# First weights in row halves, PSUM banks permuted, decode steps and x casts shared out anew

## What is computed

```
attn = einsum('ds,td->st', w1, w2) * sparse_mask
x = layernorm(x + gelu(x @ attn + b2))                 # exact gelu
e = norm(x, axis=-1);  mask = e > 64
y = where(mask, x @ W8.T, x @ W4.T) + bias             # W4, W8: weights decoded from bit planes by a table
x = layernorm(x + y)
```

## Time and profile before

| | us |
|---|---|
| median of 3 runs | 336.0 (335.06 to 337.29) |
| the profiled execution's own time | 336.07 |
| its span, first to last instruction | 334.3 |
| PE busy in it | 301.7 (90%) |
| DVE busy | 194.5 (58%) |
| ACT busy | 185.5 (55%) |
| POOL busy | 104.3 (31%) |
| granted PE clock, mean | 0.956 of full |

### The profile page before, as it was taken

How to read it: one execution, slowest core, us unless ns; L and a number is a source line. 1 busy time by engine, 2 the same in 40 slices (tenths; PEclk the granted TensorE clock), 3 DMA queues, 4 the chain that set the end, 5 groups by cost and what they waited for, 6 DMA issues and landing times.

```text
span 334.3 us, 5046 instructions
## 1 busy us (share of the span) xinstructions
PE 301.7 (90%) x1907; PEld 263.6 (79%) x1907; DVE 194.5 (58%) x347; ACT 185.5 (55%) x246; POOL 104.3 (31%) x179
## 2 busy tenths in 40 slices
PE   5899478989996779999999999999999999999970
PEld 2788375656664579999999999999999878878870
DVE  0668857436879577889966766640315434534361
ACT  1656653447887967897857887942124545121210
POOL 3000000322323237779888630000013232322220
PEclk9899877999997959999999999999999999999996
DMA  7999616799987592000111111111905877444232
GB/s 246 371 384 361 225 60 220 223 228 296 218 139 128 80 158 56 32 33 31 38 43 33 38 45 35 60 47 36 304 10 190 259 267 237 176 147 159 94 125 73
DMA packets 27183, 49.35 MB, mean 148 GB/s; under 512 B 2320, under 2 KB 11792, under 8 KB 27152
## 3 DMA queue, kind: packets, MB, share of 16 engines
q1 hardware_dynamic: 22800, 40.56, 35.0%
q0 software_dynamic: 4352, 8.39, 14.7%
HBM read 36.36 MB, written 12.58 MB: 146 GB/s over the span
## 4 chain that ended last, share of the span: by engine, by line
PE 64%; issue 12%; SPq 6%; POOL 6%; DMA 4%; DVE 3%; ACT 2%; POOLq 0%; DVEq 0%
PE acc L536 18%; PE acc L538 18%; PE acc L537 18%; POOL z L1329 5%; PE acc L519 4%; DMA q_low<-in_qbits 4%; SPq L250 3%; PE acc L461 2%; PE acc L451 1%; PE acc L415 1%; ACT x_hi L666 1%; SPq L254 1%; PE acc L431 1%; PE acc L433 0%; PE acc L432 0%
## 5 line engine op out<-in xcount | busy, mean ns | idle before, releaser
L536 PE MATMUL acc<-lin,zz 128*128 128x256 f32 (+2 forms) x424 | 130.9, 309 | 0.3 <-POOL lin L1337 0.3
L538 PE MATMUL acc<-lin,zz 128*128 128x256 f32 (+2 forms) x424 | 130.3, 307 | 0.0
L537 PE MATMUL acc<-lin,zz 128*128 128x256 f32 (+2 forms) x424 | 130.1, 307 | 0.0
L536 PEld LDWEIGHTS acc<-lin,zz 128*128 128x128 f32 x424 | 80.7, 190 | 4.7 <-issue 0.6
L537 PEld LDWEIGHTS acc<-lin,zz 128*128 128x128 f32 x424 | 80.8, 191 | 4.0
L538 PEld LDWEIGHTS acc<-lin,zz 128*128 128x128 f32 x424 | 80.7, 190 | 4.1
L692 ACT ACTIVATE leaf<-planes,lut,flip 128x1024 f32<-128x1024 uint8 x56 | 67.6, 1234 | 0.0
L948 DVE COPY_PREDICATED leaf<-planes,leaf 128x1024 f32<-128x1024 uint8 x32 | 43.1, 1346 | 12.5 <-ACT leaf L692 12.0
L1329 POOL DMA_DIRECT2D z<-in_xr x16 | 19.7, 1257 | 97.3 <-ACT z L674 97.3
L785 ACT ACTIVATE junk<-rows,cols 128x1024 bf16<-128x1024 f32 x15 | 17.2, 1149 | 41.3 <-POOL cols L1303 41.3
L415 PE MATMUL acc<-w,w 128*128 128x272 f32 (+1 forms) x128 | 31.5, 412 | 4.1 <-DMA w<-in_w1b 4.1
(11 more groups left out here) (105 smaller groups left out, 429.8 us busy)
## 6 DMA issues: line engine op xcount, KB each, us to landing
z<-in_xt SPq DMA_DIRECT2D x16, 512.0 KB, 8.8
z<-in_xr POOLq DMA_DIRECT2D x16, 512.0 KB, 6.9
out_rows<-rows SPq DMA_DIRECT2D x15, 512.0 KB, 2.9
w<-in_w2b SPq DMA_DIRECT2D x4, 1024.0 KB, 9.9
w<-in_w1b SPq DMA_DIRECT2D x8, 512.0 KB, 9.4
out_rows<-parts SPq DMA_DIRECT2D x32, 128.0 KB, 1.8
rows<-out_rows SPq DMA_DIRECT2D x16, 256.0 KB, 2.8
off_band<-in_mask_rest SPq DMA_DIRECT2D x8, 448.0 KB, 4.2
```

Source lines behind the costliest of these rows:

```text
L536: nc.tensor.matmul(bank, hi, w_hi, start=k == 0, stop=False)
L537: nc.tensor.matmul(bank, hi, w_lo, start=False, stop=False)
L538: last = nc.tensor.matmul(bank, lo, w_hi, start=False, stop=k == KB - 1)
```

## The change

**Loads (SP).** The first w2 part and w1 block 0 are each loaded in two halves by rows of the reduction (d 0 to 3, then 4 to 7), and strip 0 begins its first four products on the first halves. Between the halves stand the code bits of four blocks (256 KB, before: two blocks, 128 KB), the tables and b2. The first band half moves behind w1 block 1. The x pairs and the group-0 edge rows change their order; the loads of group 1 no longer wait for the masks, and those of groups 2 and 3 wait for the last strip alone. For this the band, the excess operands and the warm-up tile move in SBUF, from the place of z to that of `lin`; so the writes into `lin` (ACT, DVE, POOL) now wait until the masks and `mix_e` are done.

**PSUM.** UNIT_BANKS is (4, 5, 6, 7, 0, 1, 2, 3), STRIP_BANKS (2, 3). Units 0 and 1 now have the Gram banks, units 4 to 7 the banks of the linear parts. `turn(1)` uses banks 6 and 7.

**PE's order.** The excess strip comes before strip 7. Group 0 of the mix has the same order as the others; only its units 4 and 5 wait for `lin_lo` of block 0. `turn(1)` stands behind the whole mix. Then come the squares of three tiles, not one, before the first part; the squares of tile j+1 still precede part j from j = 2 on.

**ACT and DVE.** x casts of pairs 0 and 2 of group 0 go to DVE too; parts of group 0's x work move in between strips 5, 6 and 7. In the mix, the casts and decode steps stand at fixed places behind certain gelus. Counts:

| decode steps | before | after |
|---|---|---|
| among the strips | 22 | 24 |
| in the mix | 12 | 9 |
| first pass over the tiles | 32 | 33 |
| second pass | 31 | 30 (the last of before does nothing) |
| z pairs split in the mix | 6 | 4 |

The core of the diff, the counts and banks first:

```diff
-    STATS_AHEAD = 1
+    STATS_AHEAD = 3
-    EARLY_STEPS = [5, 2, 2, 2, 2, 3, 3, 3]
-    UNIT_STEPS = [n % 2 for n in range(18)] + [1, 1, 1, 0, 0, 0]
-    FIRST_STEPS = [2] * TILES
+    EARLY_STEPS = [6, 3, 3, 3, 3, 3, 2, 1]
+    MIX_STEPS = [(2, 1), (2, 1), (1, 0), (2, 0)]
+    MIX_Z = {2: ((0, 0), (0, 1)), 3: ((0, 2), (0, 3))}
+    FIRST_Z = [((1, 0), (1, 1)), ((1, 2),), ((1, 3),)] + [((2 + n // PAIRS, n % PAIRS),) for n in range(2 * PAIRS)] + [()] * 5
+    FIRST_STEPS = [1] + [2] * 11 + [3, 2, 3, 2]
...
-    TURN_IN_FIRST = {4: 2, 9: 3, 15: 4}
+    TURN_IN_FIRST = {5: 2, 11: 3, 15: 4}
...
-        UNIT_BANKS, GRAM_BANKS, SUM_BANK = (0, 1, 2, 3, 4, 7, 5, 6), (4, 5), 7
-        STRIP_BANKS, EXCESS_BANK = (5, 6), 7
+        UNIT_BANKS, GRAM_BANKS, SUM_BANK = (4, 5, 6, 7, 0, 1, 2, 3), (4, 5), 7
+        STRIP_BANKS, EXCESS_BANK = (2, 3), 7
```

SP, at the start:

```diff
+            load_first(slice(0, KB // 2), w_first)
+            load_q(0, slice(0, HALF_BLOCKS))
+            sp.dma_start(lut[:, :, :], lut4).then_inc(tables_loaded, 16)
+            sp.dma_start(b2[:, :], b2c).then_inc(tables_loaded, 16)
+            load_first(slice(KB // 2, KB), w_loaded[0])
+            load_w2(1)
+            load_w1(1)
+            load_band(0)
+            load_w1(2)
```

PE:

```diff
             for b in range(KB):
                 strip(b)
                 if b == TURN_AFTER_STRIP:
-                    turn_early(0)
-            excess_strip()
...
+                    pe.wait_ge(consts_made, 4)
+                    turn(0)
+                    excess_strip()
...
+            pe.wait_ge(gelu_done, KB * (GROUPS - 1) + 4)
+            turn(1)
```

ACT, in the mix:

```diff
+            for g in range(GROUPS):
+                gelu(g, 0)
+                done = decode_steps(MIX_STEPS[g][0], done)
+                if g + 1 < GROUPS:
+                    make_xe_hi(g + 1)
+                gelu(g, 1)
+                if g + 1 < GROUPS:
+                    make_x_hi(g + 1, 1)
+                gelu(g, 2)
+                gelu(g, 3)
+                for pair in MIX_Z.get(g, ()):
+                    make_z_hi(*pair)
+                done = decode_steps(MIX_STEPS[g][1], done)
+                gelu(g, 4)
+                gelu(g, 5)
+                if g + 1 < GROUPS:
+                    make_x_hi(g + 1, 3)
+                gelu(g, 6)
+                if g + 1 == GROUPS:
+                    make_lin_hi(1)
+                gelu(g, 7)
```

DVE, among the strips and behind them:

```diff
             for b in range(KB):
+                done = decode_steps(EARLY_STEPS[b], done)
                 mask_strip(b)
                 if b:
                     make_mix_lo(b - 1)
+                if b == KB - 3:
+                    make_x_lo(0, 0)
+                if b == KB - 2:
+                    make_xe_lo(0)
+                    make_mix_e()
+                    make_x_lo(0, 1)
             make_mix_lo(KB - 1)
+            make_x_lo(0, 2)
             make_lin_lo(0)
             make_x_lo(0, 3)
```

More of the change, by code:

```diff
@@ L287, in _ @@
             sp.dma_start(band_e[0:EXCESS, :, :, :], mask_e).then_inc(e_loaded, 16)
+            load_x(0, 0)
             load_xe(0)
-            load_q(1, slice(2, KB))
-            for r in range(1, PAIRS):
+            load_x(0, 1)
+            load_q(1, slice(HALF_BLOCKS, KB))
+            for r in range(2, PAIRS):
                 load_x(0, r)
[L292 to L296, removed]
+            for r in range(PAIRS):
                 load_x(1, r)
             load_xe(1)
+            sp.wait_ge(mix_made, KB)
             for g in range(2, GROUPS):
@@ L707, in make_lin_hi @@
                 q, c = divmod(b, 2)
+                if b == 0:
+                    act.wait_ge(masked, KB)
+                    act.wait_ge(e_made, 1)
                 if q >= 2:
@@ L720, in decode_step @@
                     centre(b - 1)
-                elif i == 10 and b >= 2 and b - 1 not in LATE:
+                elif i == 10 and b >= 3 and b - 1 not in LATE:
                     make_lin_hi(b - 1)
@@ L733, in make_z_hi, with decode_steps @@
                                      ACT.Copy).then_inc(z_hi_made, 1)
+            def decode_steps(count, done):
+                for n in range(done, done + count):
+                    decode_step(n)
+                return done + count
             done = 0
             for b in range(KB):
-                for _ in range(EARLY_STEPS[b]):
-                    decode_step(done)
-                    done += 1
+                done = decode_steps(EARLY_STEPS[b], done)
+                if b == KB - 2:
+                    make_x_hi(0, 1)
@@ L740, in _ @@
                 make_mix_hi(b)
-            for r in range(PAIRS):
-                make_x_hi(0, r)
-                if r == 1:
+                if b == KB - 3:
                     make_xe_hi(0)
+            make_x_hi(0, 3)
             make_lin_hi(0)
[L746 to L765, removed]
+            for g in range(GROUPS):
+                gelu(g, 0)
[18 more added lines that the diff above has]
+                gelu(g, 7)
@@ L925, in make_planes @@
             def make_planes(b, part):
-                if b in (0, 2) and part == 0:
-                    dve.wait_ge(q_loaded[b // 2], 16)
+                if b in (0, HALF_BLOCKS) and part == 0:
+                    dve.wait_ge(q_loaded[b // HALF_BLOCKS], 16)
                 if b >= 2 and part == 0:
@@ L1334, in _ @@
                     add_x(g, r)
-            pool.wait_ge(mix_made, KB)
+            pool.wait_ge(masked, KB)
+            pool.wait_ge(mix_e_step, 4)
             nc.gpsimd.memset(lin[:, 0, 0, :, QUARTER:WIDE].bitcast(f32), 1.0).then_inc(ones_made, 1)
```

141 lines of the change are left out of this document (53 added, 88 removed).

## The result

The changed kernel takes 320.39 us (median of 4 runs, 319.89 to 322.0), the kernel before 336.64 beside it (335.06 to 338.91). The ratio is 0.9521, with a 95% interval from 0.9454 to 0.9587: 16 us less, where 319.4 was forecast. The profiled execution took 319.89 us with a span of 318.1 (before 334.3) and a mean PE clock of 0.978 of full.

What follows compares the result with a forecast made beforehand. PE's matmuls bound the linear stage; before it PE waits on DVE's and ACT's order. A 17.2 us lead less 0.5 given back makes 16.7 off 336.07: 319.4 us, range 315.5 to 326.5.

Steps and rivals of the forecast that it cites:

- First weights and the decode's start: First loads: q lands at 6.5 us, 1.8 us earlier; strip 1 starts 0.8 us earlier, at 13.0.
- Strips paced by DVE: Strips: masks pace them, gaps of 0.3 to 1.5 us before strips 3 to 6; PE through at 44.2 us, before 47.98.
- Group 0: First mix group: waits of 1.4 us for mix_e, then for lin_lo(0) until 53.3; ends at 61.8 us, before 66.72.
- Groups 1 to 3: Rest of the mix: no stall, 13.2 us each, 39.6 together, so the mix ends at 101.4 us.
- Mix to linear: Between the mix's end and part (0, 0): 4.85 us, so that part starts at 106.2; PE's lead 17.2 us.
- Linear: Linear stage: moved z work gives 0.5 us back before squares(4); PE otherwise dense, tail as before.
- Strips and group 0 (1): Rival: strips and group 0 come out 3 to 6 us later through handovers or clock; 324 us, chance 0.15.
- The clock (4): Rival: new gaps keep the clock down in strips 3 to 7; about 20 us more, 339 us, chance 0.04.
- The early loads (5): Rival: early loads do nothing, every mask 1.7 us later; 321 us, no chance of its own, inside the forecast's.
- The mix (2): Rival: groups 1 to 3 still stall, idle 1.27, 0.24 and 3.45 us, 1.7 at lower clock; 326 us, chance 0.10.
- Rival 3: Rival: z work moved into the linear stage stalls tiles 2 to 8 by 3.5 us; 322.5 us, chance 0.09.

Runs made afterwards that it cites:

- Loads whole: Changed kernel with the first w2 part and w1 block loaded whole, first loads in their order of before, code bits still four blocks: 322.46 us.
- the spare matmuls: Changed kernel with five matmuls of the warm-up tile, results unused, between strip 0 and strip 1: 320.69 us.
- mix_hi a strip later: Changed kernel with ACT making mix_hi of strip b-1, not b, behind the decode steps of strip b: 318.15 us.
- Behind the mix: Changed kernel with DVE reading the first Gram product before lin_lo(1), POOL's memsets behind add_x(1, 0), and FIRST_STEPS altered: 319.3 us.
- the old order: Changed kernel with ACT's and DVE's order in the mix as before the change, keeping its 9 steps and 4 z pairs: 324.21 us.
- The two combined kernels: Changed kernel with mix_hi a strip later and the edits of Behind the mix: 316.99 us; the second also moves two decode steps into groups 2 and 3: 312.99 us.

## Why the prediction was right

The time and most places came out. The mechanism is the one forecast: PE's waits ahead of the linear stage go, because DVE and ACT do the urgent work first. That the total lies within 1 us is partly luck, since terms with errors of either sign cancel. And of the signs named for the strips and group 0, several came out against the forecast. The clock in the strips was 0.92, under the 0.95 named as a sign of being wrong. Of the gaps before strips 3 to 6 only one was there. The wait for `lin_lo(0)` was 0.5 us, not 2. Point by point:

| event, us | forecast | measured |
|---|---|---|
| q lands (first planes) | 6.5 | 6.92 |
| ACT's first leaf | 8.8 | 9.19 |
| strip 1 starts | 13.0 | 13.65 |
| strip 6 starts | 35.3 | 35.43 |
| last strip through | 44.2 | 44.3 |
| unit 4 of group 0 | 53.3 | 53.80 |
| group 0 through | 61.8 | 61.58 |
| groups 1 to 3, each | 13.2 | 12.9 to 13.0 |
| mix through (M) | 101.4 | 100.41 |
| part (0, 0) (T) | 106.2 | 105.66 |
| span | 317.6 | 318.1 |

**First weights and the decode's start**: right in kind. The halves brought strip 1 nothing, 13.65 against 13.74 of before, where the step had 13.0; the first bytes came later than 372 GB/s gave. Whole, 1.5 MiB were in at 7.87; in halves, with q and the tables between, 1.82 MiB at 9.42, where 0.33 MB more at 372 GB/s would be 8.8: the pieces lost some 0.6 us (an estimate from two single executions; in the other profiled runs with halves strip 0 began its second half at 9.29 to 10.08). The Trainium skill (DMA: Bandwidth & Descriptors, section Bandwidth) has small transfers less efficient; the sign agrees here, over the first microseconds alone. *Loads whole* shows that the early loads are worth 2.1 us, and the spare matmuls that strip 1's start and clock are worth none.

**Strips paced by DVE**: right, masks 0 to 5 each within 0.3 us. Of the gaps forecast before strips 3 to 6 only the last is there, 1.25 us for 1.4 (mask 4 at 35.2 less strip 5's end, by the forecast's times), because strip 1 came 0.65 us late and ran at a clock of 0.54 (13.65 to 17.40 us); the masks were not touched by it. The forecast put nothing for the clock there. By its own times PE was to be idle for 3 us before strip 1 (10 to 13.0), more than the 2.75 us that its rows show followed by the lower clock; its rival on the clock looked at the gaps made by masks alone. The slack of the strips made up for it. That it is a chain of ACT and DVE in turn, not DVE's work alone, mix_hi a strip later shows.

**Group 0**: `mix_e` at 47.0 for 46.4 and lin_lo(0) at 53.7 for 53.3, 0.6 and 0.4 us late. The clock was mis-sized. The sum had 0.7 us for it behind unit 4, but there it was 1.00 and the rest of the group took 7.8 us, as at full clock. It fell ahead of unit 4 (0.75 from 47.1 to 53.8 us), where PE would have waited for `lin_lo(0)` in any case; that is why the wait was 0.5 us and not 2. In *Behind the mix* the clock stayed up there, and the wait was 2.01 us. So the 0.7 us cover `lin_lo(0)`'s delay, and that is luck.

**Groups 1 to 3**: right that no stall stays. 13.2 was read with small handovers in it; it took 12.94 on average, 0.8 us less over the three.

**Mix to linear**: 5.25 us for 4.85. The wait for the read of the first Gram product is there (0.79); the memsets were done in time by 0.6 us, and with one Gram product only they end the wait, 1.48 us.

**Linear**: the 0.5 us given back are 0.8, in two waits for z pairs. From T to DVE's first read behind PE's last part I had 195.4 us by my terms; it took 196.2 (105.66 to 301.83). Some 0.3 us of the difference are the larger waits; the other 0.5 stay unexplained. The tail took 16.3 us, not 16.0. Together these 1.1 us are where the sum was short; part (0, 0) was 0.5 us early, and the span came out 0.5 us longer.

**Rivals.** Strips and group 0 (1) are not late as a whole: group 0 ended at 61.58 for 61.8. The clock (4) did fall in strip 1, behind 2.19 us without weights, and cost nothing, since the masks were later; behind the gap that a mask made, 1.25 us, it was 1.00, as it was with the four such gaps of *Loads whole*. The early loads (5) are worth a little more than it said, 2.1 us for 1.7. The mix (2) has no stall, and about 1.9 us of its 5.0 come back with the old order. Rival 3's waits are 0.8 us.

The parts do not add to the 16 us: undone alone, the banks cost 10.8, the mix order 3.8 and the loads 2.1; for the Gram products and the casts no difference is shown. That makes 16.7, but the near agreement means nothing: the banks' figure holds for the new order of units alone. PE's order (the excess strip before strip 7, group 0's units, `turn(1)` behind the mix) and the order of the x loads were not undone.

## What to carry to other kernels

When PE is dense in its last stage, look only at what stands ahead of it, and follow two engines' programs to the first product that waits: here the eleven figures of the table came within 1 us from durations of the old trace, though the clock inside a stage did not. Let the accumulator banks that late work needs be the first emptied, and those that early work still holds be the last filled. With PE's new order, banks in order cost 10.8 us; with another order of units the price may be another. Where two engines take turns in a chain, let one of them run its non-urgent part a step later (2.2 us here), and only then move work out of the chain.

## What the runs showed that I had not expected

After the same gap the clock came out either way. The two combined kernels have the same program of PE through the strips and the same idle time before strip 1. PE's timeline in the first, and in the second:

```profile
13.77 22.54 PE L426 MATMUL acc<-w,w 128*128 128x272 f32 x96 [2.67 <-DMA w<-in_w1b]
```

```profile
13.87 23.95 PE L426 MATMUL acc<-w,w 128*128 128x272 f32 x96 [2.67 <-DMA w<-in_w1b]
```

Six strips took 22.54 us in the one and 23.95 in the other; at the upper level throughout, as in the earlier trace rows, it is 22.27. What came before was not quite alike: the first half of strip 0 took 3.03 us in the first and 1.62 in the second. But that does not decide it. In *Behind the mix* strip 0's halves took 1.62 us each, as in the second, the gap was 2.65 us, and strips 1 to 3 ran at the upper level, in 11.27 us. In the changed kernel strip 1 ran at 0.54 after 2.19 us of idle PE. What decides is not shown. A forecast should carry nothing to 1.7 us for such a gap here (an estimate, 23.95 less 22.27), and a kernel with slack behind it, as the changed one in its strips, does not show it in its time.
